# Moving token turns, the first query and the last two queries of the first item of a kernel's second phase

## What is computed

```python
x = x + attn(layernorm(x))          # phase A: linear attention (elu + 1) with a 3-tap conv, 16 heads
x = x + xattn(layernorm(x), ctx)    # phase B: rmsnorm, 4 query heads, 1 key/value head, rope, mask, softmax
x = x + ffn(layernorm(x))           # phases C and D: gated recurrence over 16 steps, output layer

# inside xattn, for one of the 16 items
q = rope(rmsnorm(x) @ q_w) / sqrt(128)   # 4 heads of 128
k, v = rope(rmsnorm(ctx) @ kw), rmsnorm(ctx) @ vw
p = softmax(where(mask, q @ k.T, -2.38e38))
out = (p @ v) @ out_w
```

## Time and profile before

| | us |
|---|---|
| median of 3 runs | 3030.55 |
| lowest of them | 3030.36 |
| profiled execution, its own time | 3028.35 |
| its span in the trace | 3026.6 |

### The profile page before, as it was taken

One profiled execution on the slowest core, in us unless ns is written; L12 is line 12 of the kernel. 1 busy time (PEld: TensorE's weight loads), 2 busy tenths in 40 slices (PEclk: granted clock), 3 DMA queues, 4 the chain that ended last, 5 costly groups with the idle time before them and its releaser, 6 DMA issues.

```text
span 3026.6 us, 39400 instructions
## 1 busy us (share of the span) xinstructions
PE 2983.4 (99%) x14628; PEld 2508.4 (83%) x14628; DVE 1952.0 (64%) x4095; ACT 1295.3 (43%) x2511; POOL 919.5 (30%) x681
## 2 busy tenths in 40 slices
PE   7999999999989999999999999999999999999999
PEld 6888888888868888888888878888888888888887
DVE  6888888888878888888888774323333433232455
ACT  4444444444457766767766643211112212112243
POOL 0101010101357877777777720000000000000144
PEclk9999999999999999999999999999999999999999
DMA  7777777777733334344344232111111121111486
GB/s 212 201 203 209 202 215 199 215 198 217 205 105 113 105 107 127 99 113 127 99 114 126 71 125 74 56 54 55 42 42 42 56 55 57 42 28 46 153 290 224
DMA packets 319631, 380.07 MB, mean 126 GB/s; under 512 B 15312, under 2 KB 175056, under 8 KB 319440
## 3 DMA queue, kind: packets, MB, share of 16 engines
q1 hardware_dynamic: 319440, 377.56, 43.2%
HBM read 232.80 MB, written 130.02 MB: 120 GB/s over the span
## 4 chain that ended last, share of the span: by engine, by line
PE 96%; DVE 2%; ACT 1%; issue 1%; DMA 0%; POOL 0%; SPq 0%; DVEq 0%; ACTq 0%; POOLq 0%
PE c_p L132 11%; PE c_p L131 11%; PE c_p L130 11%; PE a_p L130 6%; PE a_p L131 6%; PE a_p L132 6%; PE b_n L130 5%; PE b_n L132 5%; PE b_n L131 5%; PE b_t L1723 3%; PE d_p L131 2%; PE d_p L132 2%; PE d_p L130 2%; PE a_p L1017 2%; PE a_r L131 2%; PE a_r L132 2%
## 5 line engine op out<-in xcount | busy, mean ns | idle before, releaser
L1316 POOL TENSOR_SCALAR b_soft<-b_soft,b_one_in_sum 128x512 f32<-128x512 f32 x256 | 401.2, 1568 | 201.5 <-DVE b_one_in_sum L1520 201.3
L1997 ACT ACTIVATE c_gate<-c_p,c_bias 128x512 f32<-128x512 f32 x180 | 124.2, 690 | 682.6 <-PE c_p L132 682.6
L2027 DVE TENSOR_TENSOR c_gate<-c_gate,c_gate 128x512 f32<-128x512 f32 x64 | 44.2, 691 | 502.7 <-ACT c_gate L1997 502.7
L351 POOL TENSOR_TENSOR kept_scale<-c_ln_ve,minus_half 128x4 f32<-128x4 f32 x16 | 16.1, 1008 | 880.4 <-DVE c_ln_ve L343 880.4
L1531 DVE CUSTOM_DVE_ANT_0 b_soft<-b_l,b_mask_row 128x512 f32<-128x512 f32 x256 | 175.6, 686 | 87.9 <-issue 84.0
L351 POOL TENSOR_TENSOR a_ln_sc<-a_ln_ve,minus_half 128x4 f32<-128x4 f32 x16 | 16.3, 1017 | 629.9 <-DVE a_ln_ve L343 629.9
L1379 ACT ACTIVATE b_soft<-b_soft,b_minus_top 128x512 f32<-128x512 f32 x256 | 184.5, 721 | 44.6 <-DVE b_minus_top L1531 42.6
L649 ACT ACTIVATE a_elu<-a_p 128x512 f32<-128x512 f32 x128 | 75.6, 591 | 287.6 <-PE a_p L132 287.6
L1388 ACT ACTIVATE b_p_hi<-b_t 128x512 fp32r<-128x512 f32 x256 | 151.3, 591 | 109.9 <-PE b_t L1723 109.6
L1539 DVE TENSOR_TENSOR b_p_lo<-b_t,b_p_hi 128x512 fp32r<-128x512 f32 x256 | 175.7, 686 | 16.1 <-ACT b_p_hi L1388 14.3
L1723 PE MATMUL b_t<-ident,b_soft 128*128 128x128 f32 x1024 | 154.5, 273 | 4.9 <-POOL b_soft L1316 4.9
(11 more groups left out here) (301 smaller groups left out, 9617.6 us busy)
## 6 DMA issues: line engine op xcount, KB each, us to landing
a_mem_moving<-in_ctx SPq DMA_DIRECT2D x64, 256.0 KB, 5.2
a_mem_turned<-in_ctx SPq DMA_DIRECT2D x16, 1024.0 KB, 9.2
x<-a_mem_turned SPq DMA_DIRECT2D x16, 1024.0 KB, 7.8
a_res<-in_x SPq DMA_DIRECT2D x16, 1024.0 KB, 6.4
x<-a_res SPq DMA_DIRECT2D x16, 1024.0 KB, 5.2
b_memT_f<-x SPq DMA_DIRECT2D x16, 1024.0 KB, 7.3
b_x<-x SPq DMA_DIRECT2D x16, 1024.0 KB, 6.1
b_res<-x SPq DMA_DIRECT2D x16, 1024.0 KB, 5.5
```

The lines of the kernel that those rows point to most:

```text
L1316: pool.tensor_scalar(soft[:, at, :], soft[:, at, :], one_in_sum[:, at:at + 1], None, ALU.mult).then_inc(p_norm.sem, p_norm.unit)
L1997: act.activation(gate[j % 2][i][:, :], gating.banks[(3 * j + i) % 6][:, :], ACT.Tanh if g == "c" else ACT.Sigmoid, bias=added[:, i, j:j + ...
```

## The change

1. Phase A, first step, DVE: the low parts of Wp's chunks 0 and 1 come ahead of the norm of item 1, not behind it.
2. Phase B, step 0, PE: `turn_x` 0 and 1 follow output 0 in slot 3, `turn_x` 2 and 3 follow output 1 in slot 4, `queries(0)` comes in slot 5 and outputs 2 and 3 in slot 6. `turn_x(3)` waits for the low part of chunk 0 and `queries(0)` for that of chunk 2, whose banks they take.
3. The steps of query 0 on ACT, POOL and DVE come in slots 8 to 10, not 10 to 12; the residuals in slots 5, 7, 8, 9; the low parts of item 1's memory that DVE makes in slots 10 and 11, not 14 and 15.
4. Queries 2 and 3 of item 0 go to step 1: `queries(2)` in slot 0 between the logits and `keys_values(0)`, `queries(3)` in slot 3 between the logits and `keys_values(1)`. Their steps on ACT, POOL and DVE come in slots 1 to 6 of step 1.

The other 15 items keep their order. The core of the diff:

```diff
# phase A, DVE
                     if after and old is None:
+                        weight_low(WP, 0)
                         for t in range(T):
                             self.norm_tile(dve, N, after, x, t)
                         self.norm_variance(dve, N, after)
                     if after:
                         self.norm_apply(dve, N, after, x, N.scale, N.rstd)
                     if new:
-                        weight_low(WP, 0)
                         weight_low(WP, 2)
# phase B
+            def goes_late(item):
+                return item is not None and item.b == 0
# POOL
+                        if goes_late(old):
+                            if j == 1:
+                                query_sin(old.b, 2)
+                            if j == 3:
+                                query_low(old.b, 2)
+                            if j == 4:
+                                query_sin(old.b, 3)
+                            if j == 6:
+                                query_low(old.b, 3)
-                            if j == 10:
+                            if j == (8 if goes_late(new) else 10):
                                 query_sin(new.b, 0)
+                            if goes_late(new) and j == 10:
+                                query_low(new.b, 0)
# ACT
+                            if goes_late(old):
+                                if j == 1:
+                                    query_swap(old, 2)
+                                if j == 3:
+                                    query_high(old.b, 2)
+                                if j == 4:
+                                    query_swap(old, 3)
+                                if j == 6:
+                                    query_high(old.b, 3)
-                            if j == 10:
-                                query_swap(0)
+                            if j == (8 if goes_late(new) else 10):
+                                query_swap(new, 0)
+                            if goes_late(new) and j == 10:
+                                query_high(new.b, 0)
# DVE
-                        if after and j >= 14:
-                            memory_low(after, j - 12)
+                        if after and (10 <= j < 12 if goes_late(new) else j >= 14):
+                            memory_low(after, 2 + j % 2)
+                            if goes_late(old):
+                                if j == 1:
+                                    query_cos(old, 2)
+                                if j == 2:
+                                    query_add(old.b, 2)
+                                if j == 4:
+                                    query_cos(old, 3)
+                                if j == 5:
+                                    query_add(old.b, 3)
+                            if goes_late(new):
+                                if j == 8:
+                                    query_cos(new, 0)
+                                    self.a_last_residual(dve, 2)
+                                if j == 9:
+                                    query_add(new.b, 0)
-                        if s == 0 and 4 <= j <= 7:
-                            self.a_last_residual(dve, j - 4)
+                        if s == 0 and j in (5, 7, 9):
+                            self.a_last_residual(dve, {5: 0, 7: 1, 9: 3}[j])
# PE
                     def turn_x(c):
                         bank = bank_of(OUT + c)
+                        if c == C - 1:
+                            pe.wait_ge(xT_lo.sem, xT_lo.upto(new.b, 0))
+                        if goes_late(item) and h == 0:
+                            pe.wait_ge(xT_lo.sem, xT_lo.upto(0, 2))
+                        if goes_late(old) and j == 0:
+                            queries(2, item=old)
+                        if goes_late(old) and j == 3:
+                            queries(3, item=old)
-                        if s == 0 and 3 <= j <= 6:
-                            self.a_last_output(pe, j - 3)
-                        if new and new.b == 0 and 3 <= j <= 6:
-                            turn_x(j - 3)
+                        if goes_late(new):
+                            if j == 3 or j == 4:
+                                self.a_last_output(pe, j - 3)
+                                turn_x(2 * (j - 3))
+                                turn_x(2 * (j - 3) + 1)
+                            if j == 5:
+                                queries(0)
+                            if j == 6:
+                                self.a_last_output(pe, 2)
+                                self.a_last_output(pe, 3)
-                        if new and j == 9:
+                        if new and not goes_late(new) and j == 9:
                             queries(0)
-                        if new and j == 12:
-                            queries(2)
+                        if new and not goes_late(new):
+                            if j == 12:
+                                queries(2)
```

## The result

| | before | after |
|---|---|---|
| median, us | 3029.08 (11 runs) | 3037.17 (11 runs) |
| profiled execution | 3028.35 | 3038.19 |
| its span | 3026.6 | 3036.5 |

The ratio is 1.0025, with a 95% interval of 1.0015 to 1.0034: 7.6 us slower, within 2%. One of the eleven executions of before took 5046.9 and is not in the ratio. The forecast was +4.0 with a range of -4.5 to +9.5.

The account below looks back on a forecast made before the run. PE was taken as the bound, busy 2983.4 of 3026.6 us, with only idle time and slow clock to win. Phase A's -2.3 and phase B's +6.25 gave +4.0 on the median 3030.55: 3034.5 us, range 3026 to 3040.

Parts of the forecast that it names:

- part 1: Phase A: Wp's low part ahead of the norm removes PE's 2.03 us wait and half clock: -2.3 us net.
- part 1 brings nothing: Rival, phase A: the shuffled load lands 2 us later than reckoned, no gain: 3036.5 us; chance 0.1.
- Parts 2 and 3: Phase B, steps 0 and 1: the reordered work and moved queries cost +6.25 us, bounds +0.6 to +9.
- Step 0: Phase B: PE idles about 2 us ahead of `queries(0)`, about 6 ahead of logits 2; +0.4, and +1.0 for clock.
- Port contention: Phase B, step 0: three DVE pieces beside POOL products ahead of `masked` 0 take +1.3 us.
- Half clock behind the long wait: Phase B: PE runs at half clock after idling about 6 us ahead of logits 2: +1.7 us.
- Step 1: Phase B: `queries(2)` adds +0.9 us; a 0.9 wait and `queries(3)` of 2.75 start slot 4 another 3.65 later.
- the slack: Phase B, step 1, slots 4 to 7: of PE's 3.9 us softmax waits 1.8 is usable: -1.8 us.
- the loop: Phase B, step 1, slots 5 to 8: DVE's turns of x set the time; four rounds of about 4 us, unchanged.
- Filled gaps: Rival, step 1: the queries lie in PE's waits and delay nothing else: 3026.5 us; chance 0.2.
- No half clock: Rival, phase B: no half clock behind the long idle times, the rest as forecast: 3032 us; chance 0.25.
- Half clock stays: Rival, step 1: PE meets slot 8's `encode` at half clock, again at slot 9: 3038.5 us; chance 0.1.

Follow-up runs that it names:

- e1: Kernel before with only phase A's edit, the low parts of Wp's chunks 0 and 1 ahead of item 1's norm: ratio 0.9998, -0.6 us.
- e3: Kernel before with Wp's low parts made between the norm's variance and its application, where DVE waits for POOL's power: ratio 0.9984, -4.8 us.
- e10: e2 with query 2 alone ahead of logits 2, query 3 left in slot 3 of step 1: ratio 1.0011, +3.3 us against before.
- e2: Changed kernel with phase A's edit undone, so only phase B's edits: ratio 1.0024, +7.3 us against before.
- e9: e2 with PE's idle time ahead of logits 2 filled by unused repeats of query 2's products: ratio 1.0017, +5.2 us against before.
- e7: e3, e4 and e5 together, Wp's low part in the norm's gap, queries first, memory low parts late: ratio 0.9986, -4.2 us against before.
- e6: e2 with the keys turned in slot 6, ahead of outputs 2 and 3, not in slot 7: ratio 1.0012, +3.6 us against before.
- e8: e7 with the keys also turned ahead of outputs 2 and 3, as in e6: ratio 0.9985, -4.5 us against before.
- e4: e2 with queries 2 and 3 both ahead of logits 2, where PE idled: ratio 1.0004, +1.2 us against before.
- e5: e2 with DVE making the memory's low parts again in slots 14 and 15: ratio 1.0014, +4.2 us against before.

## Why the prediction was right or wrong, point by point

The sign and the range held: +7.6 against +4.0, within +9.5. The size was off mainly in one part, the gain of part 1.

**Part 1, forecast -2.3, measured about 0.** The removed wait, the full clock and the price on DVE were right in kind. The step that failed is the landing of the last load of x, put at 55.8: in after DVE began the squares at 58.93. "Now it waits for ACT's high part of chunk 0 until 37.5": in after, the low parts began at 39.25. Of these 1.75, 0.7 is the later start of this execution, and 1.0 is ACT, which squares the memory ahead of the high parts and waited 0.85 for its DMA. That wait doesn't come with the edit: in e1 ACT doesn't have it, the low parts began at 38.31, and the squares still had to wait until 57.88. Then "the last is issued 1.9 later and lands some 4.6 after that": 4.6 was the median of four loads, and the last one is what DVE waits for. In before the last was issued at 47.0 and took 5.8, so its own trace puts the landing 0.8 later than the sum did. In after the four issues took 2.28 in place of 1.91, and all were issued by 53.28; DVE could begin at 58.93, 5.65 after that (2.71 and 5.1 in e1). The rest of the sum (55.8 to the attention) held: 58.93 to 65.00 is 6.1, against an estimated 6.3. And PE's idle time, forecast at 1.8 and "half clock may come", became 4.0, after which it did come. This is the rival *part 1 brings nothing*: the load lands later than reckoned. It had a chance of 0.1. One of the prediction's signs of being right failed here: the attention came at 65.0 and not at about 62. In e1 little or nothing is left, and e3 shows that the place ahead of the norm is the cause.

**Parts 2 and 3, forecast +6.25, measured +7.7** (T0 to T1, after less before, profiled executions). With the spread of 1.7 of this measure the two can't be told apart. The stretches of the path, each with its terms of the sum:

| stretch | before | after | difference | forecast |
|---|---|---|---|---|
| T0 to `masked` 0 | 26.38 | 27.07 | +0.7 | +0.4, and +1.0 for clock |
| `masked` 0 to the first `turn_p` | 6.16 | 9.90 | +3.7 | +0.9 +1.7 |
| first to fourth `turn_p` | 6.25 | 10.14 | +3.9 | +3.65 |
| fourth `turn_p` to first turn of x | 7.27 | 6.69 | -0.6 | -1.8 +0.8 |
| first turn of x to T1 | 15.27 | 15.24 | 0.0 | -0.4 |

- *Step 0.* Logits 0 were forecast for 867.5. They came at 868.56, less the shift of 1.0 of T0: 867.6. PE's wait ahead of `queries(0)` was 1.9 (forecast 2), for logits 2 6.45 (forecast about 6). The profile names no releaser for the first; it ended at 856.48, and DVE's low part of chunk 2 at 856.38. No half clock followed it in this execution. It did in e10 (0.66 over 855 to 860; from T0 to logits 0 21.3, against 19.75 in after). In e2 there was half clock in step 0 too (0.57 over 849 to 853, 20.4), but ahead of that wait, and e1 has it at the same place with phase B unchanged (0.57). So the wait alone didn't decide it, and an average of 1.0 was somewhat high.
- *Port contention* was underrated, at +1.3 for three pieces. The mask took 1.52 beside POOL and 0.42 in before, where POOL was idle; the two memory low parts 1.71 and 1.14 in place of 0.68. That is 2.6 for three pieces. The total hid it: from the end of the keys' low part to `masked` 0 the prediction had 9.5 with its 1.3 of contention, and 9.15 were measured with 2.6 of it, so the rest of that chain had been reckoned 1.6 too long. That `masked` 0 came out near its forecast is luck: two errors cancelled.
- *Half clock behind the long wait* was put at 1.7, from stretches of 4 to 5 us. In after it lasted from about 872.3 to 882.5, part of it while PE still idled, and cost 2.7 of the path by e9's rows: 7.17 without it is +1.0, where the forecast had +0.9. In e2 it lasted from about 873.3 to 880.1 and cost 1.8. So the term was right for the one execution and 1.0 too small for the other, and a single profile can't tell which is usual. Before had itself a stretch as long as that of e2, at about 892 to 898.6, which the prediction didn't use for its price.
- *Step 1* was right within 0.4: the two queries and their wait cost 3.9, the slack gave back 0.6 in place of 1.0, the loop kept its length.
- *The rivals.* Filled gaps fell: `masked` 0 was not early, and even when it was (e7, 25.1 after T0, 1.3 earlier than before) phase B came out even at best. No half clock fell by the windows, and e9 bounds its price. Half clock stays: it ended before slot 4 of step 1, and over 884 to 900 the granted clock was 1.00.

The rule of the Trainium skill (page SBUF — State Buffer, section "SBUF: two separate sides"), by which the loser of the port pair blocks for the whole instruction, was weighed down for the 0.1 that `query_add` lost beside a normalise. The rows of after side with it beside POOL's two-input products: the low part of 867.25 lasted until POOL's product of 867.12 and about its own 0.68 had passed. In e6 the order was the other way round, and it was POOL's product that took longer. Rule and rows differ by the kind of POOL's instruction: beside the normalise, with one large input, hardly anything is lost.

**What stays open.** The rest of the program was 1.2 longer in after, with a stretch at half clock near 1797. Such a stretch stands between 1780 and 1802 in e1, e2, e3, e6, e7, e8 and e10 too, and not in before, e4, e5 and e9; e1 and e3 have phase B unchanged, so it doesn't go with that part of the change; why it comes was not tried. Why the last load took longer in after is open as well. The memory's store issued right behind it (53.33) is not enough as a cause: in e3 the store was issued as close behind (47.42), and the largest of the four times was 5.9, against 5.8 in before and 6.2 in after.

## What to carry to other kernels

When a piece of work is moved ahead of another on an in-order engine, follow what the delayed one issues to the last DMA of the group, with the time of its last member and not the median, and look for a place where the engine stands idle on a short round trip: there the same piece was free, and some 4 us lay between the two places by the ratios. An idle time of PE that was filled cost double here when its filler was moved behind the instruction that waits: once as the idle time, and again as the filler's own time later on, with half clock on top. Put a filler ahead of the waiting instruction in the queue.

## What the runs showed of the hardware

- The length of the half-clock stretch is not fixed: some 3.5 us at 42 of before, and behind the same idle time of 6.5 some 7 us in e2 and 10 us in after, beginning while PE was still idle. Filled with unused matmuls, the same place ran at full clock (1.00 in e9, 0.79 in e2, 0.68 in after over 868 to 884), and the path was 1.8 and 2.7 shorter. An idle time of 1.84 ahead of T0 was followed by half clock in e1 and e2 (0.57 over 849 to 853), one of the same length in after was not.
- DVE and POOL slow each other by the kind of the instruction and by which began first. A one-input DVE piece (the mask, from uint8) took 0.42 with POOL idle and 1.44 to 1.52 when POOL's two-input product had begun before it; a two-input piece went from 0.68 to 1.71. Where DVE's piece began first (e6, by 0.1), it took its 0.68 and POOL's product went from 1.29 to 1.74. The normalise on POOL took 1.57 beside DVE work, and DVE's product beside it 0.79.
- Of four loads of 256 KB issued one behind the other, each took longer from issue to landing: 3.2 for the first and 5.8 for the last in before, 4.0 and 6.1 in after.
